# Second norm of a fused attention and LoRA-MoE kernel: one ScalarE instruction and a trip through DRAM in place of sixteen 32-row blocks

## The reference

```
x = x + softmax(norm(x) ctx^T / sqrt(1024), masked) ctx      # ctx: 64 rows per batch
n = norm(x)
logits = n router^T                                           # 8 experts
gate   = weights of the two best experts, from their softmax, made to sum to 1
x = x + n W^T + 2 * sum over experts e of gate_e (n A_e^T) B_e^T
```

## Time and profile before

| what | us |
|---|---|
| time, median of 3 runs (lowest, highest) | 1129.3 (1128.3, 1129.88) |
| span of the profiled execution | 1126.4 |
| PE busy | 1067.7 (95%) |
| DVE busy | 922.1 (82%) |
| ACT busy | 709.8 (63%) |
| POOL busy | 262.0 (23%) |
| DMA, mean over the span | 100 GB/s |

### The profile page before, as it was taken

The page is one execution under the profiler, slowest core; times in us unless marked ns, Lnnn a source line. Parts: engine busy times, 40 slices in busy tenths (PEclk is TensorE's granted clock), DMA queues, the critical chain, the costliest instruction groups (busy, mean ns, idle before and its releaser), DMA issues.

```text
span 1126.4 us, 20668 instructions
## 1 busy us (share of the span) xinstructions
PE 1067.7 (95%) x6160; PEld 1031.1 (92%) x6160; DVE 922.1 (82%) x2744; ACT 709.8 (63%) x1406; POOL 262.0 (23%) x286
## 2 busy tenths in 40 slices
PE   2699999999999999999999999999999999999998
PEld 2599999999999999999999999999999999999998
DVE  6988888888878888788878888788887888887874
ACT  5766765666766666666656667557666657756652
POOL 4522230222320232220322212222221222311200
PEclk9999999999999999999999999999999999999999
DMA  9222322412323312422213322223322323323200
GB/s 309 94 87 92 113 106 83 140 58 92 112 95 122 112 57 94 135 99 94 93 77 122 112 94 93 86 93 112 112 83 105 101 77 112 112 81 107 75 38 38
DMA packets 34588, 113.16 MB, mean 100 GB/s; under 512 B 4672, under 2 KB 7744, under 8 KB 34496
## 3 DMA queue, kind: packets, MB, share of 16 engines
q1 hardware_dynamic: 34496, 112.31, 29.2%
HBM read 78.74 MB, written 33.55 MB: 100 GB/s over the span
## 4 chain that ended last, share of the span: by engine, by line
PE 73%; DVE 16%; issue 8%; DMA 1%; ACT 1%; DVEq 0%; SPq 0%; POOL 0%; POOLq 0%
PE base_ps L767 21%; PE base_ps L769 20%; PE base_ps L768 20%; DVE xn L624 4%; PE ro_ps L806 3%; PE ro_ps L807 3%; PE s_ps L784 2%; PE s_ps L785 2%; DVE stats L563 2%; PE h_ps L829 1%; DVE x L610 1%; DMA w_raw<-in_wT 1%; DVE gate_b L674 1%; DVE h L679 1%; DVE top_at L652 1%
## 5 line engine op out<-in xcount | busy, mean ns | idle before, releaser
L457 ACT ACTIVATE xn<-x,shift,rstd 32x256 f32<-32x256 f32 x768 | 458.5, 597 | 262.5 <-POOL shift L374 244.1
L767 PE MATMUL base_ps<-w_hi,xT_hi 128*128 128x386 f32 (+1 forms) x1536 | 539.2, 351 | 1.5 <-DVE w_lo L278 1.4
L769 PE MATMUL base_ps<-w_hi,xT_lo 128*128 128x386 f32 (+1 forms) x1536 | 520.8, 339 | 0.0
L768 PE MATMUL base_ps<-w_lo,xT_hi 128*128 128x386 f32 (+1 forms) x1536 | 520.6, 339 | 0.0
L767 PEld LDWEIGHTS base_ps<-w_hi,xT_hi 128*128 128x128 f32 x1536 | 289.9, 189 | 9.7 <-issue 1.6
L768 PEld LDWEIGHTS base_ps<-w_lo,xT_hi 128*128 128x128 f32 x1536 | 290.5, 189 | 2.7
L769 PEld LDWEIGHTS base_ps<-w_hi,xT_lo 128*128 128x128 f32 x1536 | 289.8, 189 | 0.0
L360 POOL TENSOR_TENSOR rstd<-var_eps,neg_half 128x1 f32<-128x1 f32 x128 | 71.1, 555 | 820.1 <-DVE var_eps L568 820.1
L563 DVE BATCH_NORM_STATS2 stats<-x 128x6 f32<-128x512 f32 x256 | 164.1, 683 | 13.6 <-issue 11.4
L378 POOL TENSOR_TENSOR xT_lo<-xT_raw,xT_hi 128x1024 fp32r<-128x1024 f32 x62 | 147.4, 2398 | 0.0
L641 DVE TENSOR_TENSOR xT_lo<-x2T,xT_hi 128x512 fp32r<-128x512 f32 x128 | 82.7, 687 | 45.7 <-ACT xT_hi L463 45.7
(11 more groups left out here) (72 smaller groups left out, 985.9 us busy)
## 6 DMA issues: line engine op xcount, KB each, us to landing
xT_raw<-in_xT SPq DMA_DIRECT2D x64, 512.0 KB, 5.8
x<-in_x SPq DMA_DIRECT2D x64, 512.0 KB, 3.3
out<-x SPq DMA_DIRECT2D x64, 512.0 KB, 2.6
ctx_raw<-in_ctx SPq DMA_DIRECT2D x16, 256.0 KB, 4.8
w_raw<-in_wT SPq DMA_DIRECT2D x2, 1544.0 KB, 11.4
ctxT_raw<-in_ctxT SPq DMA_DIRECT2D x8, 256.0 KB, 4.5
w_raw<-in_wT SPq DMA_DIRECT2D x1, 1552.0 KB, 11.7
b_raw<-in_bT SPq DMA_DIRECT2D x1, 512.0 KB, 16.1
```

Of the source, the lines that this page charges most:

```text
L457: act.activation(xn2[a * QP:(a + 1) * QP, g, :], x[rows, slot(tile), a * DQ:(a + 1) * DQ], ACT.Identity, bias=shift2[rows, :], scale=rstd2 ...
L767: pe.matmul(out_, a_hi, w_h, start=start, stop=False, skip_group_check=again)
L768: pe.matmul(out_, a_hi, w_l, start=False, stop=False, skip_group_check=again)
L769: return pe.matmul(out_, a_lo, w_h, start=False, stop=stop, skip_group_check=again)
```

## The change

`norm2` on ACT is one instruction over the whole tile, 128x1024, into a new tile `xn`; the norm instructions of DVE are gone. SP stores `xn` to a DRAM tensor (`xn_out`) and, when it has landed, loads it back as four column blocks into `xq`, now in the layout for transposing (`xq_in`). DVE transposes with two instructions of twice the size, which wait for the four loads. On SP, `xn_out` and `xq_in` of the tile two ahead stand around the store of the finished tile, and the load of `xT` stands behind them. On ACT, `norm2` now comes ahead of `xT_high`. `h_transpose` stands behind the first chunk of group 2 in every step, and `e_transpose` two chunks later. POOL does the first norm's `rstd` between the two halves of `xT_low`. `b_raw` shares its memory with a slot of `x`, so its loading order at the start differs.

```diff
+            def xn_out(tile):
+                sp.wait_ge(xn_done, count(tile, 1, 1))
+                sp.dma_start(xn_dram, xn[:, :]).then_inc(xn_stored, 16)
+
+            def xq_in(tile):
+                sp.wait_ge(xn_stored, count(tile, 16, 16))
+                for a in range(Q):
+                    sp.dma_start(xq[a * QP:(a + 1) * QP, :, :],
+                                 xn_dram[:, a * DQ:(a + 1) * DQ].rearrange("(g n) e -> n g e", n=QP))\
+                      .then_inc(xq_loaded, 16)
...
             load_x((0, 2))
+            xn_out((0, 0))
+            xq_in((0, 0))
+            sp.wait_ge(b_split, 1)
             load_x((0, 3))
+            xn_out((0, 1))
+            xq_in((0, 1))
 
             def step(tile):
                 b, j = tile
+                if exists(after(tile, 2)):
+                    xn_out(after(tile, 2))
+                sp.wait_ge(out_done, count(tile, G, FREE + G))
+                sp.dma_start(out[b * TPB + j], x[:, slot(tile), :]).then_inc(stored[slot(tile)], 16)
+                if exists(after(tile, 2)):
+                    xq_in(after(tile, 2))
                 if j % 2 == 0 and exists(after(tile, 4)):
                     sp.wait_ge(xT_split, pairs(tile, 2, 2))
                     load_xT(after(tile, 4))
-                sp.wait_ge(out_done, count(tile, G, FREE + G))
-                sp.dma_start(out[b * TPB + j], x[:, slot(tile), :]).then_inc(stored[slot(tile)], 16)
                 if exists(after(tile, XS)):
...
-            def norm2(tile, g):
-
-                rows = slice(g * QP, (g + 1) * QP)
-                if g == 0:
-                    act.wait_ge(shift2_done, count(tile, 1, 1))
-                for a in range(DVE_Q, Q):
-                    act.activation(xn2[a * QP:(a + 1) * QP, g, :], x[rows, slot(tile), a * DQ:(a + 1) * DQ],
-                                   ACT.Identity, bias=shift2[rows, :], scale=rstd2[rows, :]).then_inc(xn2_act_done, 1)
+            def norm2(tile):
+                act.wait_ge(shift2_done, count(tile, 1, 1))
+                act.wait_ge(x2T_done, count(tile, TS))
+                act.activation(xn[:, :], x[:, slot(tile), :], ACT.Identity, bias=shift2[:, :],
+                               scale=rstd2[:, :]).then_inc(xn_done, 1)
...
                 nxt, nxt2 = after(tile, 1), after(tile, 2)
+                if exists(nxt):
+                    norm2(nxt)
                 if j % 2 == 1 and exists(after(tile, 3)):
                     for i in range(2):
                         xT_high(after(tile, 3), i)
...
+            def x2_transposes(tile, i):
+
+                dve.wait_ge(xq_loaded, count(tile, 16 * Q, 16 * Q))
+                out_ = x2T[:, :, :].rearrange("p c (g n) -> p g c n", n=QP)
+                dve.transpose(out_[:, i * QS:(i + 1) * QS],
+                              xq[:, i * QS:(i + 1) * QS, :].rearrange("p g (c n) -> p g c n", n=QP)).then_inc(x2T_done, 1)
...
+                base(tile, 2, range(1))
                 h_transpose(tile)
-                c = 2 if j % 2 == 0 else 5
-                base(tile, 2, range(c))
+                base(tile, 2, range(1, 3))
                 if exists(nxt2):
                     e_transpose(nxt2)
-                base(tile, 2, range(c, c + 2))
+                base(tile, 2, range(3, 5))
                 if exists(nxt2):
                     readout(nxt2)
-                base(tile, 2, range(c + 2, C))
+                base(tile, 2, range(5, C))
```

More of the change, by code:

```diff
@@ L33, in xattn_lora_moe_kernel @@
     bT_in: bass.AP,
+    xn_dram: bass.AP,
     out: bass.AP,
@@ L60, in xattn_lora_moe_kernel @@
     DQ = D // Q
-    DVE_Q = 1
-    ACT_Q = Q - DVE_Q
+    TS = 2
+    QS = Q // TS
     EPS = 1e-5
@@ L131, in xattn_lora_moe_kernel @@
         x = sb("x", [P, XS, D])
-        xn2 = sb("xn2", [P, Q, D // Q])
+        b_raw = x[:, XS - 1, :]
+        xn = sb("xn", [P, D])
+        xq = sb("xq", [P, Q, DQ])
         xT_raw = sb("xT_raw", [P, 2, C, T2])
@@ L256, in xattn_lora_moe_kernel @@
         shift2_done = sem("shift2_done")
-        xn2_act_done = sem("xn2_act_done")
-        xn2_dve_done = sem("xn2_dve_done")
+        xn_done = sem("xn_done")
+        xn_stored = sem("xn_stored")
+        xq_loaded = sem("xq_loaded")
         x2T_done = sem("x2T_done")
@@ L313, in _ @@
             load_w(1)
[L314 removed]
+            sp.dma_start(b_raw, bT_in).then_inc(b_loaded, 16)
             sp.wait_ge(w_split[0], WPARTS)
@@ L385, in step @@
                 if j % 2 == 1 and exists(after(tile, 3)):
-                    for i in range(2):
-                        xT_low(after(tile, 3), i)
+                    xT_low(after(tile, 3), 0)
                 if exists(after(tile, 2)):
                     norm1(after(tile, 2))
+                if j % 2 == 1 and exists(after(tile, 3)):
+                    xT_low(after(tile, 3), 1)
+                if exists(after(tile, 2)):
                     norm2(after(tile, 2))
@@ L485, in step @@
                     ctx_high(b + 1)
[L486 to L492, removed]
+                gate_exp(tile)
+                if j % 2 == 0 and exists(nxt2):
+                    sT_copy(nxt2)
                 if exists(nxt2):
@@ L518, in _ @@
                 xT_high((0, 2), i)
[L519 to L522, removed]
+            norm2((0, 0))
+            softmax_exp((0, 1))
             eT_copy((0, 1))
@@ L711, in step @@
                 if exists(nxt):
-                    x2_transposes(nxt, range(Q - 1))
+                    x2_transposes(nxt, 0)
                 if exists(nxt2):
@@ L715, in step @@
                 if exists(nxt):
-                    x2_transposes(nxt, range(Q - 1, Q))
+                    x2_transposes(nxt, 1)
                 hT_low(tile)
@@ L746, in _ @@
             softmax_scores((0, 1))
-            for g in range(Q):
-                norm2((0, 0), g)
             softmax_split((0, 1))
-            x2_transposes((0, 0), range(Q))
+            for i in range(TS):
+                x2_transposes((0, 0), i)
             x2T_low((0, 0))
@@ L921 @@
     out = nc.dram_tensor("out", (B * S // P, P, O), mb.dt.float32, kind="ExternalOutput").ap()
-    xattn_lora_moe_kernel(nc, *args, out)
+    xn_dram = nc.dram_tensor("xn_dram", (P, D), mb.dt.float32, kind="Internal").ap()
+    xattn_lora_moe_kernel(nc, *args, xn_dram, out)
     r = run_bass_kernel_spmd(nc, [{f"in_{n}": a for n, a in arrays.items()}], core_ids=[0])
```

15 lines of the change are left out of this document (3 added, 12 removed).

## The result

The changed kernel takes 1445.4 us (median of 4 runs, 1442.9 to 1447.7) against 1129.6 us for the kernel before beside it: a ratio of 1.279, with a 95% interval of 1.278 to 1.281. It is 28% slower. The forecast was 1382 us, 1310 to 1450. Its span is 1443.7 us.

A forecast was written before the change was run, and what follows sets the result against it. PE, busy 95% of the span, was taken as the bound. Per pair 7.45 + 1.9 - 0.84 = 8.5 us, 255 us over 30 pairs; span 1126.4 + 255 - 2 = 1379.4, median 1382 us, range 1310 to 1450 (own range 1325 to 1415).

The forecast's parts named there:

- so they can't begin before the tile has been stored, fetched back and followed by 1 MB of xT: ACT's xT casts wait behind the round trip in odd steps; PE then waits 7.45 us for h, 30 times.
- Rival 3: xT loads on SP's queue stay hidden, leaving only the 0.84 us gain per pair: 1103 us; chance 0.04.
- rival 2: Odd steps: the DMA burst runs faster and the clock hardly falls, 5.3 us per pair, 1286 us; chance 0.11.
- Rival 1: Even steps wait too, 1.7 us more in each of 32: 1436 us; chance 0.18 with other slower cases to 1500.
- the nil that was reckoned: Even steps' margin at PE's e_transpose: split done at 598.65, PE due at 598.8, so it just fits.
- store of `xn` to first `xq` load: SP's queue, odd step: the store issued at 607.0 lands, and the first xq load goes at 609.8; 2.80 us.
- first `xq` issue to cast of the second half: DMA burst of 1.5 MB, xq then xT, issued from 609.8 and ending at 618.0, before ACT's second cast.
- exponential to `h`: DVE's chain from the gate's exponential to h in odd steps: 1.84 us, read from the last step, where it was 3.99.
- PE's wait for `h`, mean of 30: PE arrives at 613.80, h reaches it at 621.25: a wait of 7.45 us in 30 odd steps.
- clock and `e_transpose` together: PE after each long wait: lowered clock or early meeting of e_transpose, 1.9 us, ends 0.7 and 3.5.
- old waits that go: PE's steady-state waits for h and e_split, 25.9 us over 31 pairs, 0.84 us per pair, nearly all removed.
- per pair: Net loss per pair of steps: 7.45 + 1.9 - 0.84 = 8.5 us, 30 pairs giving 255 us.

The follow-up runs named there:

- e1: Changed kernel with SP's xT loads moved back ahead of xn_out: 1142.5 us, ratio 1.012 to the kernel before.
- e2: As e1, and on ACT the two xT casts stand ahead of the norm again: 1128.6 us, ratio 0.999 to the kernel before.
- e7: As e2, and on PE in odd steps four chunks in place of two between h_transpose and e_transpose: 1119.9 us, ratio 0.991 to the kernel before.
- e3: Changed kernel with POOL in odd steps doing the first norm's rstd, then waiting for h_done before both xT_low halves: 1430.6 us, ratio 1.268 to the kernel before.
- e4: Changed kernel with 56 extra unread matmuls ahead of the transpose of h in the 30 odd steps loading xT: 1456.1 us, ratio 1.288 to the kernel before.
- e5: Kernel before with only h_transpose, e_transpose and readout placed on PE as in the change: 1135.2 us, ratio 1.006 to the kernel before.
- e10: Changed kernel with load_xT moved up one place on SP, ahead of xq_in: 1402.0 us, ratio 1.241 to the kernel before.

## Why the prediction was right, and where it was off

**The mechanism and the side were right.** The step "so they can't begin before the tile has been stored, fetched back and followed by 1 MB of xT" was shown by e1, which undoes nothing else and gives back 96% of the loss. Rival 3 (hidden loads) is ruled out by the cast's 298.4 us of waiting for its DMA, and rival 2 (a faster burst and a full clock) by the burst, which took its predicted length, and by the clock, which fell. Rival 1 did not occur in the changed kernel: in even steps PE waited for nothing, and DVE waited for `xq` in 7 places only. Nor did it in e1 and e2, where DVE did wait 0.7 us for `xq` in even steps and PE still waited for nothing there; it shows only where DVE's chain or the readout comes later still, at 0.33 us in e7 and 0.40 in e3. So the even steps had somewhat more room than the nil that was reckoned.

**The terms,** predicted and measured in the step shown above:

| term, us | predicted | measured |
|---|---|---|
| norm, one block | 1.24 | 1.25 |
| store of `xn` to first `xq` load | 2.80 | 2.64 |
| first `xq` issue to cast of the second half | 8.2 | 8.11 |
| norm's start to exponential | 13.36 | 12.97 |
| exponential to `h` | 1.84 | 4.11 |
| norm's start to PE's arrival | 8.11 | 7.78 |
| PE's wait for `h`, mean of 30 | 7.45 | 9.7 |
| clock and `e_transpose` together | 1.9 | 1.7 |
| old waits that go | 0.84 | 0.84 |
| per pair | 8.5 | 10.6 |

The last row is (1443.7 - 1126.4 + 2) / 30. The clock's row is the time from the odd step's `h_transpose` to the even step's, 19.13 us against 17.47 before; in e4 1.06 us of it came back where the clock stayed full.

**One term was mis-sized:** "exponential to h 1.84 us". It was taken from the last step, which has no norm but no `xT` either, so POOL is silent there. In the 30 odd steps POOL's `xT_low`, delayed by the same DMA wait, runs just then. 2.27 us in each of 30 steps are 68 us (66 with the mean of 4.02 us), and the prediction was short by 63. e3 shows the cause of the stretch: with POOL held back until `h` is done, the chain takes 1.70 us. It does not show that the time would have been 63 us less without it, since there the stretch moved and only 15 us came back.

The kernel before already had the sign of it. In the very step of rows 4 and 5, on DVE and on POOL:

```profile
609.66 0.74 DVE L654 CAST top_at<-top_at 128x2 f32<-128x2 uint32 x1
...
605.61 4.77 POOL L378 TENSOR_TENSOR xT_lo<-xT_raw,xT_hi 128x1024 fp32r<-128x1024 f32 x2
```

The cast of two columns ends at 610.40, with POOL's second subtraction (610.38). It takes 0.80 us as a mean in odd steps and 0.17 in even ones, where POOL has no `xT_low`. The 3.99 us that the prediction split into norm blocks and rest held that part as well.

**The range held with luck in it.** 1445.4 us lies near the upper end of 1310 to 1450 and outside the forecast's own 1325 to 1415. The room above was kept for rival 1 and for a dearer clock, and neither came; what filled it is POOL's stretch, which no term, rival or end of the range had. One reading of the prediction is also off without touching the sum: the queue moved 179.4 MB, 112.3 before, which is 1.6 times and not nearly twice as much.

That an instruction of VectorE with two SBUF inputs and one of GpSimd that reads SBUF exclude each other for the whole instruction is what the Trainium skill says, "SBUF — State Buffer", section "SBUF: two separate sides". The rows agree for `w_dense`, which has two such inputs: it took 2.25 us and ended with POOL's subtraction at 658.3, against 0.17 us in even steps. `top_at`, `gate` and `gate_a` were held in the same way and have one tensor input each, so that sentence does not account for them.

**The old waits went, as said,** but e5 shows that not every part had a share in it: the order on PE alone makes the kernel slower, since what it gives to `h` it takes from `e_split`. The sum had the wait for `e_split` only inside the clock's term.

## What to carry to other kernels

In an in-order queue look at what stands behind a newly placed wait before weighing bytes: two load issues moved behind a round trip cost 303 us here, and with the loads and the casts moved back (e2) the same design was level with the kernel it replaced. When a wait moves work on one engine, look at what that work then runs beside; a duration read in a quiet step isn't that of a busy one. A producer's wait for DMA (`x2_transposes`) belongs behind the short instruction that the bounding engine is waiting for (`softmax_split`): that swap alone was worth 18 to 21 us.

## What the hardware showed that I had not expected

- POOL's 128x1024 subtraction of two SBUF tiles (2.34 us) holds some small DVE instruction until it ends, and which one it is changes with the order: `w_dense` 2.25 us in the step shown of the changed kernel, `gate_a` 1.79 us as a mean in the odd steps of e1, `top_at` 1.67 in those of e2, `e_scale` 2.15 in those of e3 (all four 0.16 to 0.29 us in even steps). Not every one is held: `gate_den` and the reciprocal, with one column each, ran at 0.15 and 0.17 us beside it in the step shown.
- A mean granted clock of 0.984 in place of 0.892 (e4) made the kernel no faster. My reading is that the chain on the other engines, from the even step's `e_transpose` to the next `h` (24.5 us there, 24.15 in the changed kernel), sets the time and not PE.
- The DMA engines' share is 0.9 to 1.0 at 290 GB/s in three stretches of 2 us in e10, with stores, loads and 1 KB pieces mixed.
